# GNN and expert FFN on one core: x1 and the experts' rows loaded before the finish

## What is computed

```python
xn = _layernorm(x, axis=-1)
x = x + gnn(xn, src, dst) + mix(xn)            # x1 in the kernel
x = x + ffn(_layernorm(x, axis=-1), edge_index)
...
# ffn: a graph attention over 131072 edges scores 4 experts for each node
agg = segment_sum(h[src] * alpha, dst) + b_gat
scores = layernorm(agg).reshape(M, 4 heads, 4 experts).mean(1)
topk_s, topk_i = top_k(scores, 2)
w = softmax(topk_s)
for ei in range(4):
    g = where(topk_i == ei, w, 0.0).sum(-1)
    out = out + g * (gelu(x @ W1[ei] + b1[ei]) @ W2[ei] + b2[ei])
```

## Time and profile before

| | |
|---|---|
| time, median of 3 runs (lowest to highest) | 2785.78 us (2784.15 to 2789.37) |
| profiled execution, its time and its span | 2782.95 us, 2780.6 us |
| DVE busy | 2123.2 us, 76% of the span |
| POOL busy | 1915.5 us, 69% |
| PE busy | 1506.5 us, 54% |
| ACT busy | 1300.2 us, 47% |
| TensorE's granted clock, mean | 0.728 of full speed |
| HBM read and written | 217.05 MB, 200.79 MB |

### The profile page before, as it was taken

One profiled execution on the slowest core, in us unless ns is written; L12 is line 12 of the kernel. 1 busy time (PEld: TensorE's weight loads), 2 busy tenths in 40 slices (PEclk: granted clock), 3 DMA queues, 4 the chain that ended last, 5 costly groups with the idle time before them and its releaser, 6 DMA issues. The chain is left out here.

```text
span 2780.6 us, 23593 instructions
## 1 busy us (share of the span) xinstructions
PE 1506.5 (54%) x5746; PEld 951.1 (34%) x5746; DVE 2123.2 (76%) x3511; ACT 1300.2 (47%) x3173; POOL 1915.5 (69%) x1937
## 2 busy tenths in 40 slices
PE   2756440132323233232144199999999999995323
PEld 2523240011111111111034056566566666662123
DVE  6988769899999999998295546666666666668567
ACT  2622215799999999998043033223222232221022
POOL 1677675767677777777467677777777777777560
PEclk9878765555555555555555599999999999997566
DMA  5717664777778777775562422222222222222195
GB/s 170 235 27 210 189 213 145 255 240 253 275 230 278 255 256 267 238 255 180 161 178 71 114 34 58 59 59 56 52 53 52 53 54 66 58 56 47 48 314 218
DMA packets 224462, 419.45 MB, mean 151 GB/s; under 512 B 50698, under 2 KB 173479, under 8 KB 216902
## 3 DMA queue, kind: packets, MB, share of 16 engines
q1 hardware_dynamic: 133690, 279.68, 28.5%
q0 software_dynamic: 74480, 123.31, 19.5%
q10 hardware_dynamic: 16156, 14.98, 1.6%
HBM read 217.05 MB, written 200.79 MB: 150 GB/s over the span
## 5 line engine op out<-in xcount | busy, mean ns | idle before, releaser
L1277 POOL DMA_INDIRECT stage_got<-ffn_rows,setup_src_ffn x815 | 808.5, 992 | 248.1 <-issue 248.1
L1277 POOL DMA_INDIRECT edges_got<-gnn_rows,edges_src_gnn x644 | 610.0, 947 | 243.1 <-issue 192.5
L1391 DVE TENSOR_TENSOR_SCAN stage_y<-stage_decays,stage_y 128x960 f32<-128x960 f32 (+2 forms) x256 | 520.8, 2089 | 5.8 <-issue 5.7
L1407 ACT ACTIVATE stage_rows<-stage_y 128x3640 f32<-128x3640 f32 (+1 forms) x88 | 400.5, 4551 | 0.0
L2228 PE MATMUL stage_ph<-ffn_xt_all,stage_w 128*128 128x448 f32 x896 | 365.6, 547 | 60.4 <-ACT stage_hid L2289 29.2
L2358 DVE TENSOR_TENSOR stage_start_parts<-stage_pk,stage_of_tile 128x392 f32<-128x392 f32 x418 | 218.9, 562 | 95.2 <-PE stage_pk L2220 87.0
L2220 PE MATMUL stage_pk<-stage_start_parts 128*128 128x392 bf16 x1236 | 250.9, 341 | 63.7 <-DVE stage_start_parts L2358 51.5
L1693 PE MATMUL stage_pm<-setup_ident,stage_mix_parts 128*128 128x128 f32 x98 | 32.4, 434 | 433.6 <-ACT stage_mix_parts L1716 415.5
L1367 DVE TENSOR_TENSOR stage_y<-edges_got,stage_weights 128x896 f32<-128x896 f32 x168 | 262.6, 1667 | 0.3 <-ACT stage_weights L1346 0.3
L2228 PEld LDWEIGHTS stage_ph<-ffn_xt_all,stage_w 128*128 128x128 f32 x896 | 168.7, 192 | 195.6 <-issue 135.8
L2361 DVE TENSOR_REDUCE stage_got<-stage_start_parts 128x16 f32<-128x784 f32 x209 | 202.8, 970 | 20.1 <-issue 1.3
(11 more groups left out here) (488 smaller groups left out, 3126.0 us busy)
## 6 DMA issues: line engine op xcount, KB each, us to landing
state_gnn<-stage_rows SPq DMA_DIRECT2D x56, 1848.0 KB
y<-search_found SPq DMA_DIRECT2D x28, 896.0 KB, 4.1
tail_fin_y<-y SPq DMA_DIRECT2D x7, 3584.0 KB, 17.4
stage_got<-ffn_rows,setup_src_ffn POOLq DMA_INDIRECT x815
state_ffn<-stage_rows SPq DMA_DIRECT2D x32, 384.0 KB, 2.4
edges_got<-gnn_rows,edges_src_gnn POOLq DMA_INDIRECT x700, 3.8
staged_rows<-rows_staged SPq DMA_DIRECT2D x12, 910.0 KB, 4.7
edges_got<-staged_rows SPq DMA_DIRECT2D x6, 1820.0 KB, 13.8
```

The lines of the kernel that those rows point to most:

```text
L1277: pool.indirect_dma_start(out=got[:, u, t, :], out_offset=None, in_=self.row_dram[g.name][:, :], in_offset=bass.IndirectOffsetOnAxis(ap=sr ...
L1391: ins = dve.tensor_tensor_scan(some, r[s][:, 0:b - a, :].rearrange("p c t -> p (c t)"), some, 0.0, ALU.mult, ALU.add)
L1407: act.activation(rows[:, s, :, 0:C + H], y[:, s, :, 1:T + 1].rearrange("p c t -> p t c"), ACT.Copy).then_inc(rows_ready, 1)
```

## The change

x1 and y block 0 are loaded by SP inside the FFN loop's block, after the last store to y and before the last four chunks. y blocks 1 to 3 are loaded by SP in the carry, and blocks 4 to 6 in the finish, with four slots for y where there were three. Room is found by using buffers twice: x1 goes into the FFN's input `xt_all`, block 0 into the first half of the experts' weights, which are now one buffer `weights` that lives longer; the router's scratch tensors (`agg`, `sq`, `gate`, `rank`, `cmp`) and half of the gates go into buffers that are idle by then.

```diff
-Y_SLOTS = 3
+Y_SLOTS = 4
...
-    def carry(self, g, fin, finm, nodes=None, find=None):
+    def carry(self, g, fin, finm, nodes=None, find=None, loads=None):
...
-            if nodes is not None:
-                @block.sync
-                def _(sp):
+            @block.sync
+            def _(sp):
+                if nodes is not None:
                     nodes.sp_first(sp)
+                if loads is not None:
+                    loads(sp)
...
-            w1 = self.sb(here, "w1", [P, EXPERTS, 2, HIDDEN])
-            w2 = self.sb(here, "w2", [P, EXPERTS, FT, D])
+            w1 = self.weights[:, 0:EXPERTS * 2 * HIDDEN].rearrange("p (e k f) -> p e k f", e=EXPERTS, k=2)
+            w2 = self.weights[:, EXPERTS * 2 * HIDDEN:].rearrange("p (e f d) -> p e f d", e=EXPERTS, f=FT)
...
                 walk(step)
+                sp.wait_ge(hid_made, steps * FT)
+                self.load_x1(sp)
+                sp.wait_ge(out_made, steps * BANKS)
+                sp.wait_ge(y_out, 16 * (blocks * (EXPERTS - 1) + 1))
+                self.load_y(sp, 0)
                 for c in range(steps, FFN.chunks):
                     load_lanes(c + 2)
                     edge.sp_store(sp, c, c % 2)
...
-    def combine_buffers(self, stack):
-
-        self.fin_x = self.sb(stack, "fin_x", [P, NT, D])
-        self.fin_y = self.sb(stack, "fin_y", [P, Y_SLOTS, FFN_BLOCK, EXPERTS, D])
+    def early_buffers(self, stack, xt_all):
+
+        self.weights = self.sb(stack, "weights", [P, 2 * EXPERTS * 2 * HIDDEN])
+        self.fin_x = xt_all.rearrange("p k n -> p (k n)").rearrange("p (t d) -> p t d", d=D)
+        n = FFN_BLOCK * EXPERTS * D
+        self.fin_y = [self.weights[:, 0:n].rearrange("p (t e d) -> p t e d", t=FFN_BLOCK, e=EXPERTS)]
+        self.fin_spare = self.weights[:, n:]
         self.fin_x_in = self.sem(stack, "fin_x_in")
         self.fin_y_in = [self.sem(stack, f"fin_y_in{s}") for s in range(Y_SLOTS)]
 
+    def late_buffers(self, stack):
+
+        rest = self.sb(stack, "fin_y", [P, Y_SLOTS - 1, FFN_BLOCK, EXPERTS, D])
+        self.fin_y += [rest[:, s, :, :, :] for s in range(Y_SLOTS - 1)]
+
+    def load_x1(self, sp):
+
+        sp.dma_start(self.fin_x[:, :, :], self.x1_dram.rearrange("(t p) d -> p t d", p=P)).then_inc(self.fin_x_in, 16)
...
-    def combine_early(self, sp):
-
-        self.load_y(sp, 0)
-        sp.dma_start(self.fin_x[:, :, :], self.x1_dram.rearrange("(t p) d -> p t d", p=P)).then_inc(self.fin_x_in, 16)
+    def load_more(self, sp):
+
         for b in range(1, Y_SLOTS):
             self.load_y(sp, b)
...
-            gates = self.sb(here, "gates", [P, 2, len(BY_PE), EXPERTS, P])
+            gates = (self.sb(here, "gates", [P, len(BY_PE), EXPERTS, P]),
+                     self.found[:, 0:len(BY_PE) * EXPERTS * P].rearrange("p (n e q) -> p n e q", n=len(BY_PE), e=EXPERTS))
...
-                self.combine_early(sp)
                 for b in range(Y_SLOTS, groups):
                     sp.wait_ge(ready, b - Y_SLOTS + 1)
                     self.load_y(sp, b)
```

More of the change, by code:

```diff
@@ L2446, in finish @@
             x, yv = self.fin_x, self.fin_y
+            agg = self.edge_src["ffn"][:, 0:NT * C].bitcast(F32).rearrange("p (t c) -> p t c", c=C)
+            sq = self.fin_spare[:, 0:NT * C].rearrange("p (t c) -> p t c", c=C)
+            gate = self.fin_spare[:, NT * C:NT * (C + EXPERTS)].rearrange("p (t e) -> p t e", e=EXPERTS)
+            rank, cmp = (self.start_rows[name][:, :, :].rearrange("p t c -> p (t c)")[:, 0:NT * EXPERTS]
+                         .rearrange("p (t e) -> p t e", e=EXPERTS) for name in ("gnn", "ffn"))
             st = self.sb(here, "st", [P, NT, S])
@@ L2511, in _ @@
                         for e in range(EXPERTS):
-                            mm = pe.matmul(mixed[:, k % 4, 0:D], gates[:, b % 2, n, e, :], yv[:, s, u, e, :],
+                            mm = pe.matmul(mixed[:, k % 4, 0:D], gates[b % 2][:, n, e, :], yv[s][:, u, e, :],
                                            start=(e == 0), stop=(e == EXPERTS - 1))
@@ L2522, in spread_gates @@
                         for e in range(EXPERTS):
-                            ins = act.activation(gates[:, b % 2, n, e, :], self.ident[:, :], ACT.Copy,
+                            ins = act.activation(gates[b % 2][:, n, e, :], self.ident[:, :], ACT.Copy,
                                                  scale=gate[:, b * G + u, e:e + 1])
@@ L2643, in combine @@
                         for t in range(G - len(BY_PE)):
-                            dve.scalar_tensor_tensor(x[:, b * G + t, :], yv[:, s, t, e, :], gate[:, b * G + t, e:e + 1],
+                            dve.scalar_tensor_tensor(x[:, b * G + t, :], yv[s][:, t, e, :], gate[:, b * G + t, e:e + 1],
                                                      x[:, b * G + t, :], ALU.mult, ALU.add)
@@ L2717, in run @@
                         self.nodes_and_rows(own, own_m, xt_all, find, nodes)
+                    self.early_buffers(with_xt, xt_all[:, :, :])
+                    last, last_m = fin[:, 0:FFN.cols + H], finm
                     with ExitStack() as mine:
@@ L2720, in run @@
                         self.edge_tiles(FFN, mine)
-                        last, last_m = fin[:, 0:FFN.cols + H], finm
                         begin("stage2")
                         self.ffn_and_experts(last, last_m, xt_all, own)
+                    with ExitStack() as tail:
+                        begin("tail")
+                        self.late_buffers(tail)
                         begin("carry_ffn")
[L2725 to L2730, removed]
+                        self.carry(FFN, last, last_m, loads=self.load_more)
+                        begin("finish")
+                        self.finish(own_h, own_m, out)
 _INS = ['x', 'src', 'dst', 'L0_gnn_W', 'L0_gnn_att', 'L0_mix_Wqkv', 'L0_mix_Wout', 'L0_mix_gamma', 'L0_ffn_W_gat',
```

9 lines of the change are left out of this document (2 added, 7 removed).

## The result

The changed kernel takes 2792.09 us in the median of 11 runs (2788.74 to 2793.32). The kernel before, run beside it, takes 2785.60 (2783.62 to 2789.37). The ratio is 1.0021, with a 95% interval of 1.0012 to 1.0031: between 3.3 and 8.6 us slower. The profiled execution took 2792.72 us, its span is 2790.4; that is 9.8 us over the profiled execution of the kernel before, where the medians are 6.5 us apart.

A forecast was written before the change was run, and what follows sets the result against it. It took DVE to bound the loop's last chunks and POOL's row of gathers the finish; +2.2 + 1.5 + 3.4 - 3.4 = +3.7 us took 2782.95 to 2786.7, the median to 2789.5, range 2784 to 2796.

The forecast's parts named there:

- the likeliest case: The forecast with all terms small, +1 to +5.5 us in all, alone 2786.8 to 2791.3; chance 0.45.
- the text's edge: Whole kernel: a measurement can tell about 0.2%, 5.6 us; less counts as the same.
- Lanes later: Rival, FFN loop: gathers slow the loads, the lanes cost +5.0 for +2.2, in all +6.5, 2792.3; chance 0.25.
- the lanes: FFN loop: DVE waits for chunk 30's lanes, queued behind x1 and block 0 on SP; +2.2 us, bounds 0 and +5.0.
- the end read: Carry: POOL's first small DMA, reading the partitions' end rows, is slowed by blocks 1 to 3; +1.5 us.
- That the loads were hidden before: Finish of the kernel before: DVE waits for neither x1 nor any block of y; removing SP's 25.61 us gains nothing.
- That SP would be held: FFN loop: SP's issue of y block 0 behind x1 lasts 15 to 20 us, delaying the lanes' issue to 2539.2.
- The count of 1,840 rows: SP's queue: SP is let on at about 1,840 outstanding rows, so the carry's third block is accepted at once.
- SP held in the carry: Rival, carry: SP waits to issue the third block, the carry ends 8 us later, 2793.6; 0.1, shared with a worse write.
- Half: Carry: the read's delay taken midway between no hit and a full hit of 2.8 us, as +1.5.
- The write: Carry: POOL's second small DMA lands in 5.6 us instead of 2.2 beside the loads; +3.4 us, bounds 0 and 4.1.
- the 21st gather: Finish: with the loads gone by 2650, this state gather lands in about 2.4 us, not 5.8; -3.4 us.

The follow-up runs named there:

- experiment 8: Changed kernel with x1 and y block 0 issued behind the lanes of chunk 30, and blocks 1 to 3 at the finish's start: 2784.43 us, ratio 0.9999.
- experiment 4: Changed kernel's buffers and four slots, but all loads where they were before, at the start of the finish: 2785.52 us, ratio 1.0004.
- experiment 1: Changed kernel, but SP issues x1 and y block 0 behind the lanes of chunk 30 instead of ahead: 2786.35 us, ratio 1.0008.
- experiment 2: Changed kernel, but ACT issues the lanes of chunk 30 on its own queue: 2787.25 us, ratio 1.0006.
- experiment 5: Changed kernel, but y block 0 is issued in the finish, only x1 stays ahead of the lanes: 2787.78 us, ratio 1.0009.
- experiment 6: Changed kernel, but loop loads behind the lanes of chunk 30, blocks 1 to 3 in the finish after the 21st state gather: 2782.35 us, ratio 0.9987.
- experiment 3: Changed kernel, but y blocks 1 to 3 are issued at the start of the finish, not in the carry: 2789.41 us, ratio 1.0017.
- experiment 7: Changed kernel, but in the carry SP waits for the end rows before issuing blocks 1 to 3: 2789.42 us, ratio 1.0015.

## Why the prediction was right, and where it was short

It gave 2789.5, 0.62 for no difference above 0.2% and 0.35 for slower, in a range of 2784 to 2796. The time is 2792.09, in the range, 2.6 us above the number, and beyond the likeliest case's own 2786.8 to 2791.3. The direction is right. Which side of the text's edge, 5.6 us, the change is on stays open: against 2785.60 it is 6.5 us, with an interval of 3.3 to 8.6. The case called "Lanes later" is priced at the same +6.5, 2792.3. That the numbers meet is in part luck: it has the lanes at +5.0 where they cost 4.7, the end read at 1.5 where it cost 3.1, and its reason for the lanes isn't what the trace shows.

*That the loads were hidden before.* DVE's waits show it, and experiment 8 shows it for x1 and block 0. For y's last block the text looked at DVE alone. PE did wait for it in the kernel before:

```profile
2761.84 7.13 PE L2512 MATMUL finish_mixed<-tail_fin_y,finish_gates 128*128 128x256 f32 x24 [2.57 <-DMA tail_fin_y<-y]
```

With four slots (experiment 4 and the changed kernel) PE has no such wait. It was covered all the same: DVE waits 3.2 us for PE's products before, 3.4 in experiment 4 and 2.9 in the changed kernel.

*That SP would be held* is right for the loop, 19.66 us against some 17, and 2.78 us for the lanes as computed. The count of 1,840 rows behind it did not hold. When SP was let on at 2541.62, the engines had moved some 6.1 MB since y's last store was issued, 0.9 of them that store and 0.2 gathers: about 1.4 MB of x1 were left, 1,300 rows (an estimate from the windows). In the carry, where the count said that the third block would be accepted at once, its issue lasted 5.9 us:

```profile
2625.91 5.92 SPq L2444 DMA_DIRECT2D tail_fin_y<-y  x1
```

By then some 2.0 MB of the 7.3 of the two blocks ahead had moved, so about 1,300 rows of 4 KB were left. The three issues together took 6.95 us, not 1.5. Nothing waited for SP there, so the time doesn't feel it; of the rival "SP held in the carry" the holding came and the cost didn't.

*The lanes.* The mechanism is right (experiments 1, 2 and 5). The term, +2.2, was too small: the wait was 5.1 and the step net of the last gather 4.7. The windows of the changed kernel (first the carry's, which is used below, then three of the loop's stretch), and the landings in the view of DMAs, for x1 and block 0 in the changed kernel and for x1 in experiment 1:

```profile
2627.00:2645.00 18.00, 2.70 (x10) 1.02 (x10) 4.55 (x24) 0.72 (x3) 1.27 (x2) 0.50 1.02 407
2525.00:2532.00 7.00, 2.14 (x6) 0.74 (x6) 5.75 (x15) 1.25 (x4) 5.48 (x6) 0.58 1.04 299
2532.00:2546.00 14.00, 8.36 (x36) 3.17 (x36) 12.85 (x20) 1.68 (x3) 10.57 (x12) 0.84 1.10 335
2546.00:2556.00 10.00, 3.91 (x12) 1.43 (x12) 6.71 (x11) 0.00 (x0) 7.54 (x8) 0.70 1.04 383
...
ffn_xt_all<-x SPq DMA_DIRECT2D x1, 6272.0 KB, 26.8
nodes_gnn_weights<-y SPq DMA_DIRECT2D x1, 3584.0 KB, 35.8
...
ffn_xt_all<-x SPq DMA_DIRECT2D x1, 6272.0 KB, 24.5
```

The rates that the sum took from the finish were right: from 2532 on the loop shows 335 and 383 GB/s, the finish 334 and 387. So a steady share of the loop's gathers, the reason of the range's upper end and of "Lanes later", is not what made the lanes late. That bound had them at 2556.1, or 2558.7 on this execution's later clock, where DVE compared them at 2558.50; but its 32.5 us add 2.9 where 12.0% of 29.6 is 3.6, without the figure for the difference, and the agreement is luck. (The wait of 2.5 us is 2.4 by the text's own times.)

The shortfall lies ahead of block 0. Issued at 2521.28 and landed 26.8 us later, x1 was in at 2548.1; the sum, on the later clock, had 2544.8. Block 0 landed 9.7 us after it, as computed (9.8), and DVE compared the lanes 0.7 us behind it, less than the 1.2 allowed. Two things are in the 3.3 us. First, x1 runs into y's last store, issued 0.4 us ahead of it: in the five kernels where it does, x1 lands in 25.7 to 26.9 us and the store in 5.3; in the three where the lanes and 6 us lie between (experiments 1, 6 and 8), in 24.5 to 24.6 and 4.1. Second, even 24.5 is 1.0 more than the 23.5 that the sum has from x1's issue: it let x1 end when its bytes had moved, and allowed nothing for its landing. How the 3.3 us divide between the two was not measured further.

*The end read.* "Half" was wrong: +3.1 in place of +1.5. It was hit in full although issued only 1.3 us after SP's first load (2626.22 against 2624.89). The read takes 6.0 us, and from 2627 to 2645 the core moves 407 GB/s (the first of the windows above). Experiments 3 and 7 show that it is the loads. Half was a choice between two bounds; the upper one, 2.8, was nearly the value.

*The write* was +3.4 and *the 21st gather* -3.4; measured +3.45 and -3.37.

The two short terms make 2.5 + 1.6 = 4.1 us. The steps of the table without the first mark sum to +7.2, against +3.7 forecast; the two small negative ones at the end (-0.7) make up the rest. The medians say +6.5.

## What to carry to other kernels

A load that no engine waits for gained nothing here by being issued earlier (experiment 8); look first at what stands behind it in its queue and beside it on the engines. Look at the waits of every engine that uses the data, not of one. Count the bytes ahead of each small transfer that an engine needs soon, and put the small one first or on another queue. A bulk load that must run somewhere is placed against the small DMAs on the critical path: here the same three blocks cost 6.5 us beside the carry (3.1 for its read, 3.4 for its write), 3.4 beside the first gathers, and nothing behind them. Time a load to its landing, not to its last byte, and start the count at what its queue still holds.

## What was not expected of the hardware

Two small row DMAs of POOL beside a full load landed in 5.6 to 6.0 us in place of 2.2 to 2.4, almost at once when the load began, and whether they read or wrote. A load of 0.29 MB on ACT's queue, beside SP's full queue, landed in 6.4 us, against 3.0 in the median of the run. These small transfers lost 3.2 to 3.8 us to a stream on another queue, and the lanes lost 13.6 and more behind it on the same one. By the windows, the hold on SP's next issue ended with some 1,300 rows outstanding in the loop and in the carry of the changed kernel, and with about 1,750 (the prediction reads 1,840) in the finish of before; what sets it is open.
